# The head's second load starts with 16 rows ahead of W and the first tile: products of field pairs on one core

## The reference, cut to what matters

```python
# x: (4096, 32, 64) float32, W: (64, 64) float32
vid = jnp.einsum('bfd,de->bfe', x, W)              # each field of each sample through W
idx_i, idx_j = jnp.triu_indices(32, k=1)           # the 496 pairs i < j
return x[:, idx_i, :] * vid[:, idx_j, :]           # (4096, 496, 64) float32
```

## Time and profile before

| | |
|---|---|
| median of 3 runs | 1284.37 us (1284.08 to 1284.89) |
| profiled execution, its own time | 1283.99 us |
| span of the profiled execution | 1282.7 us |
| VectorE busy | 1077.8 us, 84% of the span |
| TensorE matmuls busy | 166.0 us, 13% |
| moved by DMA | 553.73 MB, mean 432 GB/s over the span |

### The profile page before, as it was taken

One profiled execution on the slowest core, in us unless ns is written; L12 is line 12 of the kernel. 1 busy time (PEld: TensorE's weight loads), 2 busy tenths in 40 slices (PEclk: granted clock), 3 DMA queues, 4 the chain that ended last, 5 costly groups with the idle time before them and its releaser, 6 DMA issues. The chain is left out here.

```text
span 1282.7 us, 1107 instructions
## 1 busy us (share of the span) xinstructions
PE 166.0 (13%) x256; PEld 65.1 (5%) x256; DVE 1077.8 (84%) x255; POOL 0.2 (0%) x4
## 2 busy tenths in 40 slices
PE   2030110303010020030301203002020020302000
PEld 1010000101000000010100001001000000101000
DVE  6799998989889647889999979918899898999582
POOL 0000000000000000000000000000000000000000
PEclk8565565656556556575655556556555565657555
DMA  9999999999999999999999999999999999999999
GB/s 391 433 439 435 429 437 442 429 425 441 441 425 431 439 429 433 425 446 437 425 435 443 429 425 441 436 422 433 426 431 446 429 427 446 435 427 425 448 433 394
DMA packets 10370, 553.73 MB, mean 432 GB/s; under 512 B 1152, under 2 KB 1152, under 8 KB 1152
## 3 DMA queue, kind: packets, MB, share of 16 engines
q1 hardware_dynamic: 9216, 508.56, 91.6%
q10 hardware_dynamic: 1152, 45.15, 8.3%
HBM read 33.62 MB, written 520.09 MB: 432 GB/s over the span
## 5 line engine op out<-in xcount | busy, mean ns | idle before, releaser
L194 DVE TENSOR_TENSOR mem<-mem,vid 128x2048 f32<-128x2048 f32 (+13 forms) x255 | 1077.8, 4296 | 181.6 <-DMA out_dram<-mem 151.7
L255 PE MATMUL vid<-mem 128*128 (+1 forms) x256 | 166.0, 811 | 1010.6 <-PEq L254 1010.6
L255 PEld LDWEIGHTS vid<-mem 128*128 128x128 f32 x256 | 65.1, 267 | 1110.6 <-issue 1110.6
L362 POOL MEMSET const-bfloat16-1.0<- 128x1 bf16 x1 | 0.1, 103 | 0.0
L362 POOL MEMSET const-uint8-127<- 128x1 uint8 x1 | 0.1, 102 | 0.0
L362 POOL MEMSET const-float32-0.0<- 128x1 f32 x1 | 0.1, 100 | 0.2 <-issue 0.2
L362 POOL MEMSET const-float32-1.0<- 128x1 f32 x1 | 0.1, 99 | 0.0
## 6 DMA issues: line engine op xcount, KB each, us to landing
out_dram<-mem SPq DMA_DIRECT2D x7, 7168.0 KB, 21.0
out_dram<-mem SPq DMA_DIRECT2D x4, 6144.0 KB, 20.9
mem<-in_r_x_dram SPq DMA_DIRECT2D x2, 7936.0 KB, 38.7
mem<-in_r_x_dram ACTq DMA_DIRECT2D x1, 7936.0 KB, 25.9
out_dram<-mem ACTq DMA_DIRECT2D x1, 7168.0 KB, 37.9
mem<-in_r_x_dram SPq DMA_DIRECT2D x2, 2304.0 KB, 44.0
mem<-in_r_x_dram ACTq DMA_DIRECT2D x1, 2304.0 KB, 36.9
mem<-in_L_rec_W_x_dram ACTq DMA_DIRECT2D x1, 1088.0 KB, 5.6
```

The source lines that it names most:

```text
L194: self.engine.tensor_tensor(*operands, MULT).then_inc(self.dve, 1)
L255: nc.tensor.matmul(vid[:, b * BANK : b * BANK + BANK, :], lhsT=w, rhs=mem[:, bass.ds(k * step + (first + b * BANK), BANK), :], start=True, ...
L362: nc = _bacc.Bacc("TRN2", target_bir_lowering=False, num_devices=1, dynamic_dma_scratch_size=256)
```

## The change

The head is cut at other units: 16, 62 and 98 units instead of 16, 124 and 36. The run of 62 units (units 286 to 347, tile 1 and most of tile 2) is brought by two transfers. Its first 16 rows are the kernel's very first DMA, issued on ACT's queue ahead of `x0` under a semaphore of its own, `early`. The other 112 rows are issued where the run of 124 units was, behind `x0` and the head's first run. ACT waits for `early` together with `x0` ahead of the first `go`.

```diff
-HEAD = range(6), [(16, 16), (286, 124), (410, 36)]
+HEAD = range(6), [(16, 16), (286, 62), (348, 98)]
+EARLY_RUN, EARLY = 1, 16
...
+    lo, n = HEAD[1][EARLY_RUN]
+    at = sum(m for _, m in HEAD[1][:EARLY_RUN])
+    early = load(act, mem[:EARLY, lo : lo + n, :], x[:EARLY, at : at + n, :], "early", [])
     ws = load(act, whole[:, : 1 + HALF, :], x0[:, : 1 + HALF, :], "x0", [(0, f) for f in range(HALF)])
...
-    def stretch(q, tiles, runs, name):
+    def stretch(q, tiles, runs, name, early=None):
...
-            made.append(load(q, mem[:, lo : lo + n, :], x[:, at : at + n, :], f"{name}{r}", fields(tiles, lo, n)))
+            p = EARLY if r == early else 0
+            made.append(load(q, mem[p:, lo : lo + n, :], x[p:, at : at + n, :], f"{name}{r}", fields(tiles, lo, n)))
...
-    stretch(act, *HEAD, "h")
+    stretch(act, *HEAD, "h", EARLY_RUN)
...
-            for s in [ws, *(loaded[t, b * BANK + f] for b in half for f in range(BANK))]:
+            for s in [ws, early, *(loaded[t, b * BANK + f] for b in half for f in range(BANK))]:
                 act.after(s)
```

## The result

The changed kernel takes 1292.42 us (1292.13 to 1293.30), the kernel before, measured beside it, 1284.03 us: 8.4 us more by the medians, a ratio of 1.0064 with a 95% interval from 1.0054 to 1.0074 (6.9 to 9.5 us). It is slower, as forecast, by 3.1 us more than the 5.3 us that the forecast summed up. The span of the profiled executions grew from 1282.7 to 1292.0 us.

A forecast was written before the change was run, and what follows sets the result against it. The prediction took DMA transfers at 434 GB/s as the bound. First transfer 4.1, other 112 rows 2.0 and ramp -0.8 summed to +5.3 us, giving a median of 1289.7 us, range 1283.1 to 1293.0.

The forecast's parts named there:

- What bounds the kernel: Whole run: the DMA engines at 434 GB/s; time they lose is lost to the result, VectorE's is not while transfers are queued.
- The first transfer: 16 rows of 62 fields ahead of `x0`: expected to take 5.3 us, 4.1 us above the full rate.
- the ramp: Start, 1.7 to 3.2 us, engines not all beginning together: at most 0.8 us won back by the 16 rows going first.
- The other 112 rows: Second transfer of the 62-unit run: 2.0 us more, taken between nothing and 4.1 us.
- The issues: One more issue on ACT's queue, `x0` issued about 0.4 us later: hidden by the first transfer.
- the wait for `early`: ACT ahead of the first `go`: costs one instruction, as `early` was queued ahead of `x0` and has landed.
- the cut: Head cut at 62 and 98 units: costs nothing, as tiles 1 and 3 are needed long after the loads land.
- Rival 1: First transfer runs at the full rate and fills the ramp: 1283.6 us, down to 1283.1; chance 0.34.
- Rival 2: Engines begin one after the other whatever the row count, ramp unchanged, rows at full rate: 1284.4 us; chance 0.05.
- Rival 3: 112 rows dealt out in turn, 16 neighbouring rows always written together: +32, about 1316 us; chance 0.05.
- Rival 4: VectorE starts late and transfers run dry: 1 to 3 us on top of the forecast, counted within the upper end.

The follow-up runs named there:

- late16: Changed kernel with its 16 rows issued behind `x0` and the head's first run, right ahead of the 112 rows, instead of first: 1293.38 us against 1284.22.
- two_queues: Kernel before, with the head's first run issued on SP's queue at the start instead of behind `x0` on ACT's: 1284.21 us against 1284.22.
- extra_near: Changed kernel with the 16 rows as an extra copy into free units and the run of 62 units loaded with all 128 rows: 1287.34 us against 1284.29.
- rest_7x16: Changed kernel with the 112 rows as seven transfers of 16 neighbouring rows each, one behind the other: 1313.40 us against 1283.99.
- cut_only: Kernel before with head runs of 16, 62 and 98 units, all of 128 rows, no early transfer: 1284.01 us against 1284.22.
- all_rows_first: Changed kernel with the first transfer as 8 fields of all 128 rows, head runs 16, 8 and 152: 1284.12 us against 1284.29.

## Why the prediction was right, and where a term was mis-sized

- **What bounds the kernel** was right. In `late16` and in the changed kernel the lost DMA time comes out as time of the whole, and in `two_queues` a first product that is 2.7 us later costs nothing.
- **The first transfer, +4.1 us with -0.8 for the ramp:** too high by 1.4 us. Together they came to 1.9 us (`extra_near`), not 3.3. No run shows the 0.8 us of the ramp by itself; if they are there, the price is 2.7 us, and 2.7 + 6.5 are the 9.2 us of `late16`, where nothing can be won in the ramp. Back to back the price is 3.9 us (`rest_7x16`). An overlap with the next transfer fits this: the first packets of `x0` start at about 4.8 us, while the 16 rows land only at 8.1 us (0.7 + 7.4). The sum had no such overlap.
- **The other 112 rows, +2.0 us:** this is the step that was mis-sized most, by 4.5 us, and its upper bound of 4.1 us was too low as well: 6.5 us by the difference of two runs, and 5.3 us by the rate of 264 GB/s in their stretch. I let engines meet for half of the time; whatever hinders them costs more. The share of 1.01 says that the engines had packets in hand all the time, and the 428 GB/s in `extra_near` that the same run in 128 rows is not hindered.
- **Luck.** The two misses have opposite signs: 1.4 us too much and 4.5 us too little leave 3.1. With the first term right and the second as it stood, the forecast would have been +3.9 us. The result lies 0.6 us below the upper end of the range, and that end was set for a first transfer of about 9 us, not for slow 112 rows. The bound, the direction and the two partial transfers as the cause were right by argument; that the number lies in the range is in part luck.
- **The issues, the wait for `early`, the cut:** nothing that shows, as costed (`cut_only`, `all_rows_first`).
- **Rival 1** (full rate) is out: the 16 packets took 3.6 us each instead of 1.17, and its point of decision, 3.4 us in all above the full rate, was exceeded by the 112 rows alone. **Rival 2** is out too: the 16 packets start within 0.75 us, and not at the full rate. **Rival 3** is what `rest_7x16` does, +29 us; the changed kernel is far from it, so the 112 rows are not dealt out in that order. **Rival 4** was not seen: from 25.9 to 40 us, where the first store is issued behind the loads, the rate is 432 GB/s.
- The price that I worked out from the Trainium skill, "SBUF — State Buffer", section "Door 1: The DMA port swizzle (why `[64,N]` ≈ `[32,N]`)", an estimate of 4.9 us for the first transfer, would have brought that term closer to what it measured, and the sum down by 0.4 us, away from the result.

What stays open is the mechanism of the 112 rows. That the transfer is slow because it does not cover all 128 rows is shown (264 GB/s, against 428 for the same run in 128 rows). That the written side is the cause was tested for the 16 rows only; for the 112 it is carried over. Whether their number counts or that they begin at row 16 was not separated, and which engine has which row the trace does not name. That pairs of engines meet on one way into the memory fits the 264 GB/s and the worse result of 48 and 64 rows, but it is argued, not shown.

## What to carry to other kernels

Where DMA is the bound, look twice at a load that is split by rows: here the 16 rows cost 1.9 us and the 112 rows that were left to a second transfer 6.5 us. To put a small piece first, cut it by fields and keep all rows, which cost nothing here (`all_rows_first`), though it won nothing either. Read GB/s, not the busy share: both stretches that lost time stood at a share of 1.0.

## What was not expected

- 112 of 128 rows moved at 264 GB/s, 61% of the full rate, at a share of 1.01; two transfers of 48 and 64 rows at 160 GB/s.
- 16 written rows eight apart landed 1.5 us sooner than 16 neighbours; the rows read made no difference.
- 16 rows of 8 KB each ahead of `x0` did not delay it (6.4 us, 6.3 before), while 16 rows of 31 KB delayed it by 4.2 us.
